# Self-attention scores of a query block: high and low keys in one TensorE product, with the low part added by ScalarE and VectorE

## The chip, the cores and the metric

The kernel runs on one core of a Trainium2 chip. The time is that of one execution on the device in microseconds (us), and the number compared is the median of several runs. The profile is of one more execution of the same program.

## The reference

One pre-norm decoder layer on x of 16 sequences of 256 tokens with 512 features: self-attention, cross-attention to a context, and a mixture of eight experts, each added to its input. The change lies in the self-attention:

```
x  = x + attn(layernorm(x), w_q, w_kv, w_dense)
q  = (x @ w_q)  as 4 groups x 4 heads x 128;   k, v = split(x @ w_kv) as 4 groups x 128
scores = q . k * 128**-0.5, causal;   probs = softmax(scores)
out = (probs @ v) @ w_dense
```

All of it is float32.

## The kernel before

`attention_phase` does the self-attention. To keep float32 accuracy with TensorE's float32r products, each operand is held as a high part (the value rounded to float32r by a ScalarE copy) and a low part (value minus high part, by VectorE), and each product is three: high·high, high·low, low·high (`product3`). The names end in `_h` and `_l`: `kT_h`, `qT_l` and so on.

The tokens go in blocks of 512, that is two sequences, and the heads in two halves. So there are 16 iterations `t`: 8 blocks with the first eight heads, then the same 8 blocks with the other eight. The first eight iterations also load the next block (`x_in`), normalise it and transpose it (`row_stats`, `mean_and_variance`, `apply_norm`, `xT_fill`). Iterations 7 ("turn") and 8 ("fresh") also load and split the second half's weights. Each iteration has 16 units `u`, a unit being one head of one sequence: 256 units in all.

A unit has 256 queries as two blocks of 128, in one PSUM bank `ps_s[u % 2]` of 512 columns. Columns 0 to 127 are the scores of the first 128 queries against the first 128 keys (the rest is masked by causality anyway), columns 128 to 383 those of the second 128 queries against all 256 keys; the last 128 columns are unused. `scores` makes six products, three of 128 columns and three of 256, and a bf16 product with an identity (line 603) that adds the causal mask to both diagonal blocks and raises `s_filled`.

Then, for unit u, on the other engines:

- VectorE, `maxima`: waits for `s_filled`; the negated row maximum of the first block (line 427) and of the second (line 428); raises `max_done`.
- ScalarE, `exponentials`: the exponentials of the first block (line 312) and of the second (line 314) from PSUM into `probs`, with their row sums.
- VectorE, `normaliser`: reciprocal of the sums (line 435), and the scaling of the first block of `probs` (line 437). GpSimd scales the second block (line 278).
- TensorE, `transposes`: `probs` is transposed into `ps_pT` (line 619) once both are scaled.
- ScalarE copies the high part `pT_h` (line 307), VectorE makes `pT_l` (line 384, of which there are several users).
- TensorE, `values_product`: for two units at a time, probabilities times values into `ps_c`; ScalarE copies `cT_h` (line 319) and VectorE makes `cT_l`.

Every engine works through its own list in the order in which the program has it. For ScalarE the body of unit u is: exponentials(u); for odd u up to 11 query ((u + 3) / 2), line 303, and for odd u from 3 context ((u − 3) / 2), line 319; then the copy `pT_h` of unit u − 1. For VectorE it is: maxima(u); in the first eight iterations a piece of the next block's layer norm (the statistics of `x_in`, line 389, in u = 3 to 6); normaliser(u); for the same odd u `qT_l` (line 420) and `cT_l`; then `pT_l` of unit u − 1; for u from 12 an add of the dense product. For TensorE it is: scores(u); half of the query projection number u // 2 + 2 while that is below 8, so for u up to 11; for odd u from 3 values_product; transposes(u − 1); for u from 12 a quarter of the dense product. After unit 15 come the keys, the values and the first two queries of the next block between the rest of the dense product, and the scores of unit 0.

So in unit u the exponentials of u are followed on ScalarE by `pT_h` of u − 1, VectorE's `pT_l` of u − 1 stands ahead of the maxima of u + 1, and these release the exponentials of u + 1.

Of the kernel before, what the change touches and what calls it, by code (L numbers as in the profile page):

```python
# [13 lines left out]
F32R = mybir.dt.float32r  # L14
BF16 = mybir.dt.bfloat16
I32 = mybir.dt.int32
ACT = mybir.ActivationFunctionType
ALU = mybir.AluOpType
AX = mybir.AxisListType

P = 128
BANK = 512
LN_EPS = 1e-5
# [11 lines left out]
def attention_phase(nc, x_rows, w_q, w_kv, w_dense, xT_pairs, x1_rows, TOKENS, HIDDEN, SEQ, HEADS, GROUPS):  # L35
# [18 lines left out]
    with ExitStack() as ctx:  # L54
        def sb(name, shape, dt=F32):
            return ctx.enter_context(nc.sbuf_tensor(name, shape, dt))
# [4 lines left out]
        def sem(name):  # L61
            return ctx.enter_context(nc.semaphore("a_" + name))
# [12 lines left out]
        acc = sb("acc", [P, TB, HIDDEN])  # L75
        xn = sb("xn", [P, TB, HIDDEN])
        xT = [sb(f"xT_{s}", [P, KT, BANK], F32R) for s in "hl"]
        kT = [sb(f"kT_{s}", [P, G, BANK], F32R) for s in "hl"]
        v = [sb(f"v_{s}", [P, TB, G * D], F32R) for s in "hl"]
        qT = [sb(f"qT_{s}", [P, 4, BANK], F32R) for s in "hl"]  # L80
        probs = sb("probs", [P, 2, 3 * P])
# [6 lines left out]
        mv = sb("mv", [P, TB, 2])  # L88
        veps = sb("veps", [P, TB])
        minus_half = sb("minus_half", [P, TB])  # L90
        negmax = sb("negmax", [P, 2, 2])
        rowsum = sb("rowsum", [P, 2, 2])
        rinv = sb("rinv", [P, 2, 2])
# [13 lines left out]
        stored = sem("stored")  # L107
        stats_done = sem("stats_done")
        aggr_done = sem("aggr_done")
        veps_done = sem("veps_done")  # L110
        rstd_done = sem("rstd_done")
        xn_done = sem("xn_done")
        xT_stored = sem("xT_stored")
        xT_loaded = sem("xT_loaded")
# [1 line left out]
        proj_high = sem("proj_high")  # L116
        proj_low = sem("proj_low")
        s_filled = sem("s_filled")
        max_done = sem("max_done")
        exp_done = sem("exp_done")  # L120
        rinv_done = sem("rinv_done")
# [79 lines left out]
        with nc.Block() as block:  # L201
# [49 lines left out]
            @block.gpsimd  # L251
            def _(pool):
                nc.gpsimd.memset(ident[:], 0.0).then_inc(consts, 1)
                nc.gpsimd.memset(causal[:], 0.0).then_inc(consts, 1)
                nc.gpsimd.memset(minus_half[:], -0.5).then_inc(consts, 1)
                pool.wait_ge(consts, 3)
                nc.gpsimd.affine_select(out=ident[:], in_=ident[:], compare_op=ALU.not_equal, fill=1.0, base=0,
                                        pattern=[[-1, P]], channel_multiplier=1).then_inc(consts, 1)

                nc.gpsimd.affine_select(out=causal[:], in_=causal[:], compare_op=ALU.is_ge, fill=NEG, base=0,  # L260
                                        pattern=[[-1, P]], channel_multiplier=1).then_inc(consts, 1)
                pool.wait_ge(consts, 5)
                nc.gpsimd.tensor_copy(ident_b[:], ident[:]).then_inc(consts, 1)

                def norm_scale(t):

                    wait_alone(pool, aggr_done, TB * (t + 1), (consts, 6))
                    nc.gpsimd.tensor_scalar(veps[:], mv[:, :, 1], LN_EPS, None, ALU.add).then_inc(veps_done, 1)
                    pool.wait_ge(veps_done, t + 1)
                    nc.gpsimd.tensor_tensor(veps[:], veps[:], minus_half[:], ALU.pow).then_inc(rstd_done, 1)  # L270

                norm_scale(0)

                def body(t, kind, half):
                    for u in range(UNITS):
                        s = u % 2
                        wait_alone(pool, rinv_done, UNITS * t + u + 1, (consts, 6))
                        nc.gpsimd.tensor_scalar(probs[:, s, P:3 * P], probs[:, s, P:3 * P], rinv[:, s, 1:2], None,  # L278
                                                ALU.mult).then_inc(probs_done, 1)
                        if u == TB + 3 and made(kind, half):  # L280
                            norm_scale(t + 1)

                pairs(body)(pool)

            @block.scalar
            def _(act):
# [18 lines left out]
                def probs_transposed(t, u):  # L305
                    act.wait_ge(pT_filled, UNITS * t + u + 1)
                    nc.scalar.activation(pT[0][:, u % 4, :], ps_pT[u % 2][:, 0:3 * P], ACT.Copy).then_inc(pT_high, 1)  # L307

                def exponentials(t, u):
                    s = u % 2  # L310
                    act.wait_ge(max_done, UNITS * t + u + 1)
                    nc.scalar.activation(probs[:, s, 0:P], ps_s[s][:, 0:P], ACT.Exp, bias=negmax[:, s, 0:1],  # L312
                                         accum_out=rowsum[:, s, 0:1])
                    nc.scalar.activation(probs[:, s, P:3 * P], ps_s[s][:, P:3 * P], ACT.Exp,  # L314
                                         bias=negmax[:, s, 1:2], accum_out=rowsum[:, s, 1:2]).then_inc(exp_done, 1)
# [19 lines left out]
                    values(0, n)  # L335
                query(0, 0)
                query(0, 1)
                exponentials(0, 0)

                def body(t, kind, half):  # L340
                    last = kind == "last"
                    for u in range(UNITS):
                        if u:
                            exponentials(t, u)
                        if u % 2 and (u + 3) // 2 < NH:
                            query(t, (u + 3) // 2)
# [25 lines left out]
                    if not last:  # L372
                        for n in range(2):
                            values(t + 1, n)
                        query(t + 1, 0)
                        query(t + 1, 1)
                        exponentials(t + 1, 0)

                pairs(body)(act)
# [2 lines left out]
            def _(dve):  # L382
# [12 lines left out]

                def apply_norm(t, n):
                    if n == 0:
                        dve.wait_ge(rstd_done, t + 1)
                    nc.vector.tensor_scalar(xn[:, n, :], x_in[:, n, :], mv[:, n, 0:1], veps[:, n:n + 1],
                                            ALU.subtract, ALU.mult).then_inc(xn_done, 1)  # L400

# [21 lines left out]

                def maxima(t, u):
                    s = u % 2
                    dve.wait_ge(s_filled, UNITS * t + u + 1)
                    nc.vector.tensor_reduce(negmax[:, s, 0:1], ps_s[s][:, 0:P], AX.X, ALU.max, negate=True)
                    nc.vector.tensor_reduce(negmax[:, s, 1:2], ps_s[s][:, P:3 * P], AX.X, ALU.max,  # L428
                                            negate=True).then_inc(max_done, 1)

                def normaliser(t, u):
# [107 lines left out]
            def _(pe):  # L539
# [50 lines left out]
                def scores(t, u):  # L590

                    m, b = unit(u)
                    g, s = m // HPG, u % 2
                    if b == 0:
                        pe.wait_ge(proj_low, FILLS * t + 8 + m + 1)
                    for qb in range(2):
                        c0, n = qb * P, (qb + 1) * P
                        q0 = b * SEQ + qb * P
                        product3(ps_s[s][:, c0:c0 + n], qT, (slice(None), m % 4, slice(q0, q0 + P)),
                                 kT, (slice(None), g, slice(b * SEQ, b * SEQ + n)), qb == 0, False)  # L600

                    diagonal = ps_s[s][:].rearrange("p (c k) -> p c k", c=BANK // P)[:, 0:3:2, :]
                    nc.tensor.matmul(diagonal, ident_b[:], causal[:, None, :].to_broadcast([P, 2, P]),
                                     start=False, stop=True).then_inc(s_filled, 1)

# [2126 lines left out]
```

## Time and profile before

| | |
|---|---|
| median of 3 runs | 2808.98 us |
| lowest and highest | 2804.44 and 2813.34 us |
| the profiled execution, its own time | 2802.59 us |
| span of its profile | 2801.0 us |
| self-attention in it | 0 to 1374 us |
| TensorE busy | 2603.9 us, 93% of the span |
| VectorE busy | 1875.0 us, 67% |
| ScalarE busy | 1455.1 us, 52% |
| GpSimd busy | 995.5 us, 36% |
| mean granted TensorE clock | 0.97 |

The engines are named in the rows as PE (TensorE's products), PEld (its weight loads), DVE (VectorE), ACT (ScalarE), POOL (GpSimd) and SP (SyncE, which issues DMAs). L427 is line 427 of the kernel. A row of the timeline has the start in us from the start of the span, the duration, the engine, the line, the operation and the tiles as output<-input, and in brackets the idle time of the engine before it and what ended that. Matmuls are pipelined: the next one starts before the shown end of the one before.

### The profile page before, as it was taken

Reading aid. Unit: us, or ns where it says so; the run is one execution under the profiler, and the core shown is the slowest. Engines: PE = TensorE matmul, PEld = TensorE weight load, DVE = VectorE, ACT = ScalarE, POOL = GpSimd, SP = SyncE. Lnnn points to the kernel's source line nnn. Section 1 sums busy time; section 2 is a strip of 40 time slices with the busy share of each in tenths; the row PEclk is TensorE's granted clock in tenths of the full one; section 3 lists DMA queues with packets and bytes.
Section 4 is the critical chain, followed back from the end, with each engine's and each line's share of the span. In section 5 each row is a group of like instructions: output and inputs, shape, how many; then the busy total and the mean of one; then the engine's idle time right before and its main releaser. Section 6 shows DMA issues by size and latency. Waiting matters only on the chain. (4 is left out here: it accounts for less than half of the span.)

```text
span 2801.0 us, 51111 instructions
## 1 busy us (share of the span) xinstructions
PE 2603.9 (93%) x15536; PEld 1816.8 (65%) x15537; DVE 1875.0 (67%) x3845; ACT 1455.1 (52%) x2868; POOL 995.5 (36%) x1178
## 2 busy tenths in 40 slices
PE   7999999999999999999759999999999986399997
PEld 6888888888888888888524444444443423277775
DVE  6556655566544455554569898889888876576665
ACT  4334433345433344333337777777777765255554
POOL 1112211112111112211235665665665647433332
PEclk9999999999999999999879999999999988699999
DMA  4102222013201111111154555555655558655554
GB/s 150 69 7 75 75 75 75 26 49 136 91 31 61 45 45 60 60 47 43 53 123 118 133 136 136 139 131 136 139 135 130 133 147 287 230 101 106 111 106 83
DMA packets 140817, 282.49 MB, mean 101 GB/s; under 512 B 39344, under 2 KB 42288, under 8 KB 135616
## 3 DMA queue, kind: packets, MB, share of 16 engines
q1 hardware_dynamic: 112416, 214.99, 26.7%
q0 software_dynamic: 23664, 58.09, 10.0%
q10 hardware_dynamic: 4656, 8.40, 1.0%
q8 instruction: 43, 0.70, 0.1%
q14 instruction: 38, 0.31, 0.0%
HBM read 147.82 MB, written 81.68 MB: 82 GB/s over the span
## 5 line engine op out<-in xcount | busy, mean ns | idle before, releaser
L1566 DVE TENSOR_REDUCE b_negmax<-b_ps_s 128x2 f32<-128x1024 f32 x512 | 611.2, 1218 | 52.9 <-PE b_ps_s L1751 46.4
L278 POOL TENSOR_SCALAR probs<-probs,rinv 128x256 f32<-128x256 f32 x256 | 242.0, 945 | 1094.3 <-DVE rinv L435 1094.3
L1366 ACT ACTIVATE b_probs<-b_ps_s 128x1024 f32<-128x1024 f32 x512 | 520.0, 1020 | 198.9 <-PE b_ps_s L1762 197.6
L312 ACT ACTIVATE probs<-ps_s,negmax 128x128 f32<-128x128 f32 x256 | 94.1, 367 | 484.5 <-DVE negmax L428 484.5
L1775 PE MATMUL b_ps_o<-b_probs,b_v_stack 128*32 128x256 f32 (+1 forms) x2816 | 295.0, 491 | 0.9 <-ACT b_probs L1366 0.8
L1762 PEld LDWEIGHTS b_ps_s<-b_stack 56*128 56x128 f32 x1024 | 96.3, 184 | 272.4 <-issue 165.7
L1762 PE MATMUL b_ps_s<-b_stack 56*128 56x512 f32 x1024 | 257.6, 500 | 15.4 <-DVE b_negmax L1566 7.5
L1751 PE MATMUL b_ps_s<-b_stack 54*128 54x512 f32 x1024 | 228.7, 443 | 42.4 <-DMA b_stack<-b_split 24.0
L543 PE MATMUL ps_proj<-xT_h,wq_h 128*128 128x512 f32 x512 | 216.0, 422 | 0.0
L2461 POOL DMA_INDIRECT out<-e_y,e_place_int x71 | 118.1, 1664 | 253.4 <-DMA out<-e_y,e_place_int 218.4
L543 PE MATMUL ps_proj<-xT_h,wq_l 128*128 128x512 f32 x512 | 201.7, 394 | 0.0
L543 PE MATMUL ps_proj<-xT_l,wq_h 128*128 128x512 f32 x512 | 200.1, 391 | 0.0
L435 DVE RECIPROCAL rinv<-rowsum 128x2 f32<-128x2 f32 x256 | 42.3, 165 | 217.5 <-ACT probs L314 217.5
L543 PE MATMUL ps_d<-wd_h,cT_h 128*128 128x512 f32 x384 | 157.6, 410 | 1.4 <-DVE cT_l L384 1.4
L1751 PEld LDWEIGHTS b_ps_s<-b_stack 54*128 54x128 f32 x1024 | 99.5, 190 | 91.6 <-ACT b_probs L1366 46.1
L543 PE MATMUL ps_s<-kT_h,qT_h 128*128 128x128 f32 (+1 forms) x512 | 156.8, 306 | 0.0
L543 PE MATMUL ps_d<-wd_h,cT_l 128*128 128x512 f32 x384 | 150.7, 392 | 0.0
L543 PE MATMUL ps_d<-wd_l,cT_h 128*128 128x512 f32 x384 | 150.0, 391 | 0.0
L543 PE MATMUL ps_s<-kT_l,qT_h 128*128 128x128 f32 (+1 forms) x512 | 142.8, 279 | 0.0
L307 ACT ACTIVATE pT_h<-ps_pT 128x384 fp32r<-128x384 f32 x256 | 127.1, 496 | 29.9 <-PE ps_pT L619 29.9
L384 DVE TENSOR_TENSOR pT_l<-ps_pT,pT_h 128x384 fp32r<-128x384 f32 x256 | 140.6, 549 | 2.5 <-ACT pT_h L307 2.5
L543 PE MATMUL ps_s<-kT_h,qT_l 128*128 128x128 f32 (+1 forms) x512 | 142.2, 278 | 0.0
(334 smaller groups left out, 6641.1 us busy)
## 6 DMA issues: line engine op xcount, KB each, us to landing
b_stack<-b_split SPq DMA_DIRECT2D x336, 128.0 KB
e_row<-rows_by_expert SPq DMA_DIRECT2D x71, 258.0 KB, 2.9
b_out_tiles<-row_sum_inverses SPq DMA_DIRECT2D x64, 256.0 KB
x<-acc SPq DMA_DIRECT2D x15, 1024.0 KB, 4.8
x_in<-in_x SPq DMA_DIRECT2D x8, 1024.0 KB, 8.1
normalised_x_split<-xT_h SPq DMA_DIRECT2D x8, 1024.0 KB, 9.8
normalised_x_split<-xT_l SPq DMA_DIRECT2D x8, 1024.0 KB, 11.0
acc<-in_x SPq DMA_DIRECT2D x8, 1024.0 KB, 11.3
```

What stands on the lines that cost most here:

```text
L278: nc.gpsimd.tensor_scalar(probs[:, s, P:3 * P], probs[:, s, P:3 * P], rinv[:, s, 1:2], None, ALU.mult).then_inc(probs_done, 1)
L307: nc.scalar.activation(pT[0][:, u % 4, :], ps_pT[u % 2][:, 0:3 * P], ACT.Copy).then_inc(pT_high, 1)
L312: nc.scalar.activation(probs[:, s, 0:P], ps_s[s][:, 0:P], ACT.Exp, bias=negmax[:, s, 0:1], accum_out=rowsum[:, s, 0:1])
L384: return nc.vector.tensor_tensor(dst, ps, h.bitcast(F32), ALU.subtract)
L435: nc.vector.reciprocal(rinv[:, s, :], rowsum[:, s, :]).then_inc(rinv_done, 1)
L543: ins = nc.tensor.matmul(out, w[a][w_at], m[b][m_at], start=st, stop=en)
L1366: nc.scalar.activation(probs[:, k % 2, p, :, :], ps[:], ACT.Exp, scale=0.25).then_inc(e_done, 1)
L1566: nc.vector.tensor_reduce(negmax[:, k, p, :], ps[:], AX.X, ALU.max, negate=True).then_inc(m_reduced, 1)
L1751: ins = nc.tensor.matmul(ps[:, i, :], stack[rows, quad, 0, p, k * P:(k + 1) * P], stack[rows, quad, 1, p, :], start=True, stop=True)
L1762: ins = nc.tensor.matmul(ps[:, i, :], stack[rows, q, 1, p, k * P:(k + 1) * P], stack[rows, q, 0, p, :], start=True, stop=True)
L1775: ins = nc.tensor.matmul(ps_o[32 * h:32 * h + 32, cols], v_stack[:, k, HQ * q + h, :], probs[:, k % 2, h // 2, h % 2, cols], start=(k == 0 ...
L2461: nc.gpsimd.indirect_dma_start(out, bass.IndirectOffsetOnAxis(place_int[i][:], 0), y[i][:], None, compute_op=ALU.add).then_inc(y_out[i], 16)
```

## The change

The high and the low keys become the two halves of one tensor, `kT_both`. For the first 128 queries the products high queries · high keys and high queries · low keys are one product of 256 columns, whose output goes to block 0 and to the unused block 3 of the bank (`blocks[:, 0:4:3, :]`). Low queries · high keys is added to block 0 as before. A score group so has five products and the mask where it had six and the mask.

The two blocks are added outside TensorE. ScalarE copies block 3 to SBUF (`by_low`) as soon as the group is done; VectorE adds it to block 0 into `first_scores_sum` in SBUF, then takes the maximum of the second block, then that of the sum; the first exponential reads the sum from SBUF and no longer PSUM. A semaphore `first_block` counts the copy and the add. VectorE waits for ScalarE's copy where it waited for TensorE. To make room for that semaphore `veps_done` and `rstd_done`, of the layer norm, become one, `rstd_step`.

```
-        kT = [sb(f"kT_{s}", [P, G, BANK], F32R) for s in "hl"]
+        kT_both = sb("kT", [P, 2, G, BANK], F32R)
+        kT = [kT_both[:, i] for i in range(2)]
...
+        by_low = sb("by_low", [P, 2, P])
+        first_scores_sum = sb("first_scores_sum", [P, 2, P])
...
+                def products_by_low(t, u):
+                    s = u % 2
+                    act.wait_ge(s_filled, UNITS * t + u + 1)
+                    nc.scalar.activation(by_low[:, s, :], ps_s[s][:, 3 * P:], ACT.Copy).then_inc(first_block, 1)
+
                 def exponentials(t, u):
                     s = u % 2
                     act.wait_ge(max_done, UNITS * t + u + 1)
-                    nc.scalar.activation(probs[:, s, 0:P], ps_s[s][:, 0:P], ACT.Exp, bias=negmax[:, s, 0:1],
+                    nc.scalar.activation(probs[:, s, 0:P], first_scores_sum[:, s, :], ACT.Exp, bias=negmax[:, s, 0:1],
                                          accum_out=rowsum[:, s, 0:1])
...
                         if u:
+                            products_by_low(t, u)
                             exponentials(t, u)
...
                 def maxima(t, u):
                     s = u % 2
-                    dve.wait_ge(s_filled, UNITS * t + u + 1)
-                    nc.vector.tensor_reduce(negmax[:, s, 0:1], ps_s[s][:, 0:P], AX.X, ALU.max, negate=True)
-                    nc.vector.tensor_reduce(negmax[:, s, 1:2], ps_s[s][:, P:3 * P], AX.X, ALU.max,
+                    dve.wait_ge(first_block, 2 * (UNITS * t + u) + 1)
+                    nc.vector.tensor_tensor(first_scores_sum[:, s, :], ps_s[s][:, 0:P], by_low[:, s, :], ALU.add).then_inc(first_block, 1)
+                    nc.vector.tensor_reduce(negmax[:, s, 1:2], ps_s[s][:, P:3 * P], AX.X, ALU.max, negate=True)
+                    dve.wait_ge(first_block, 2 * (UNITS * t + u) + 2)
+                    nc.vector.tensor_reduce(negmax[:, s, 0:1], first_scores_sum[:, s, :], AX.X, ALU.max,
                                             negate=True).then_inc(max_done, 1)
...
-                    for qb in range(2):
-                        c0, n = qb * P, (qb + 1) * P
-                        q0 = b * SEQ + qb * P
-                        product3(ps_s[s][:, c0:c0 + n], qT, (slice(None), m % 4, slice(q0, q0 + P)),
-                                 kT, (slice(None), g, slice(b * SEQ, b * SEQ + n)), qb == 0, False)
-
-                    diagonal = ps_s[s][:].rearrange("p (c k) -> p c k", c=BANK // P)[:, 0:3:2, :]
+                    blocks = ps_s[s][:].rearrange("p (c k) -> p c k", c=BANK // P)
+                    q0 = b * SEQ
+                    nc.tensor.matmul(blocks[:, 0:4:3, :], qT[0][:, m % 4, q0:q0 + P], kT_both[:, :, g, q0:q0 + P], start=True, stop=False)
+                    nc.tensor.matmul(blocks[:, 0, :], qT[1][:, m % 4, q0:q0 + P], kT[0][:, g, q0:q0 + P], start=False, stop=False)
+                    product3(ps_s[s][:, P:3 * P], qT, (slice(None), m % 4, slice(q0 + P, q0 + 2 * P)),
+                             kT, (slice(None), g, slice(q0, q0 + 2 * P)), False, False)
+
+                    diagonal = blocks[:, 0:3:2, :]
```

## Rows read from the trace of the kernel before

**Rows 1.** The page of the profiled execution, its head and its part 1.
```profile
span 2801.0 us, 51111 instructions
...
PE 2603.9 (93%) x15536; PEld 1816.8 (65%) x15537; DVE 1875.0 (67%) x3845; ACT 1455.1 (52%) x2868; POOL 995.5 (36%) x1178
...
```

**Rows 2.** Timeline, ScalarE, iteration 11: start us, us, engine, line, operation, tiles.
```profile
...
993.36 0.37 ACT L312 ACTIVATE probs<-ps_s,negmax 128x128 f32<-128x128 f32 x1 [1.48 <-DVE negmax L428]
...
994.16 0.49 ACT L307 ACTIVATE pT_h<-ps_pT 128x384 fp32r<-128x384 f32 x1
995.82 0.37 ACT L312 ACTIVATE probs<-ps_s,negmax 128x128 f32<-128x128 f32 x1 [1.17 <-DVE negmax L428]
...
996.62 0.59 ACT L303 ACTIVATE qT_h<-ps_proj 128x512 fp32r<-128x512 f32 x1
...
999.57 0.37 ACT L312 ACTIVATE probs<-ps_s,negmax 128x128 f32<-128x128 f32 x1 [1.48 <-DVE negmax L428]
...
```

**Rows 3.** Timeline, VectorE, the same stretch.
```profile
...
994.71 0.55 DVE L384 TENSOR_TENSOR pT_l<-ps_pT,pT_h 128x384 fp32r<-128x384 f32 x1
995.17 0.28 DVE L427 TENSOR_REDUCE negmax<-ps_s 128x1 f32<-128x128 f32 x1
995.37 0.41 DVE L428 TENSOR_REDUCE negmax<-ps_s 128x1 f32<-128x256 f32 x1
...
997.25 0.69 DVE L420 SCALAR_TENSOR_TENSOR qT_l<-ps_proj,qT_h 128x512 fp32r<-128x512 f32 x1
997.86 0.68 DVE L384 TENSOR_TENSOR cT_l<-ps_c,cT_h 128x512 fp32r<-128x512 f32 x1
998.46 0.55 DVE L384 TENSOR_TENSOR pT_l<-ps_pT,pT_h 128x384 fp32r<-128x384 f32 x1
998.92 0.28 DVE L427 TENSOR_REDUCE negmax<-ps_s 128x1 f32<-128x128 f32 x1
...
```

**Rows 4.** Timeline, TensorE, the products of u = 12 and the next transposes.
```profile
...
1009.20 0.31 PE L543 MATMUL ps_s<-kT_h,qT_h 128*128 128x128 f32 x1
1009.35 0.27 PE L543 MATMUL ps_s<-kT_l,qT_h 128*128 128x128 f32 x1
...
1009.57 0.34 PE L543 MATMUL ps_s<-kT_h,qT_h 128*128 128x256 f32 x1
1009.74 0.28 PE L543 MATMUL ps_s<-kT_l,qT_h 128*128 128x256 f32 x1
...
1009.98 0.28 PE L603 MATMUL ps_s<-causal,ident_b 128*128 128x256 bf16 x1
1010.61 0.52 PE L619 MATMUL ps_pT<-ident,probs 128*128 128x128 f32 x3 [0.35 <-POOL probs L278]
...
```

**Rows 5.** Timeline, TensorE, the mask product of u = 1.
```profile
...
976.81 0.28 PE L603 MATMUL ps_s<-causal,ident_b 128*128 128x256 bf16 x1
...
```

**Rows 6.** Timeline, VectorE, the first maximum of u = 1.
```profile
...
977.13 0.29 DVE L427 TENSOR_REDUCE negmax<-ps_s 128x1 f32<-128x128 f32 x1 [1.48 <-PE ps_s L603]
...
```

**Rows 7.** Timeline, ScalarE, exponentials of u = 1 and of u = 11.
```profile
...
977.79 0.37 ACT L312 ACTIVATE probs<-ps_s,negmax 128x128 f32<-128x128 f32 x1 [6.33 <-DVE negmax L428]
...
1008.24 0.37 ACT L312 ACTIVATE probs<-ps_s,negmax 128x128 f32<-128x128 f32 x1 [1.17 <-DVE negmax L428]
...
```

**Rows 8.** Timeline, GpSimd, the scaling of u = 11.
```profile
...
1009.52 0.94 POOL L278 TENSOR_SCALAR probs<-probs,rinv 128x256 f32<-128x256 f32 x1 [1.52 <-DVE rinv L435]
...
```

**Rows 9.** Waits of iterations 1 to 14: in total us, times, longest us.
```profile
...
DVE stats L389 <- DMA x_in<-in_x: 9.3, 6, 1.7
...
```

**Rows 10.** Timeline, ScalarE, iteration 4: exponentials of u 3 and 4.
```profile
...
389.52 0.37 ACT L312 ACTIVATE probs<-ps_s,negmax 128x128 f32<-128x128 f32 x1 [1.17 <-DVE negmax L428]
...
394.28 0.37 ACT L312 ACTIVATE probs<-ps_s,negmax 128x128 f32<-128x128 f32 x1 [2.50 <-DVE negmax L428]
...
```

**Rows 11.** Groups by shape, ScalarE: xcount, busy us, mean ns, idle before.
```profile
...
L1353 ACT ACTIVATE b_split<-b_raw_q 128x512 fp32r<-128x512 f32 x32 | 19.8, 618 | 0.7 <-DVE b_raw_q L1548 0.6
...
```

**Rows 12.** Groups by line and shape, VectorE, whole span.
```profile
...
L2198 DVE TENSOR_REDUCE r_rank<-c_above 128x32 f32<-128x256 f32 x8 | 3.4, 420 | 0.3
...
```

More of the change, by code:

```diff
@@ L109, in attention_phase @@
         aggr_done = sem("aggr_done")
-        veps_done = sem("veps_done")
-        rstd_done = sem("rstd_done")
+        rstd_step = sem("rstd_step")
         xn_done = sem("xn_done")
@@ L118, in attention_phase @@
         s_filled = sem("s_filled")
+        first_block = sem("first_block")
         max_done = sem("max_done")
@@ L267, in norm_scale @@
                     wait_alone(pool, aggr_done, TB * (t + 1), (consts, 6))
-                    nc.gpsimd.tensor_scalar(veps[:], mv[:, :, 1], LN_EPS, None, ALU.add).then_inc(veps_done, 1)
-                    pool.wait_ge(veps_done, t + 1)
-                    nc.gpsimd.tensor_tensor(veps[:], veps[:], minus_half[:], ALU.pow).then_inc(rstd_done, 1)
+                    nc.gpsimd.tensor_scalar(veps[:], mv[:, :, 1], LN_EPS, None, ALU.add).then_inc(rstd_step, 1)
+                    pool.wait_ge(rstd_step, 2 * t + 1)
+                    nc.gpsimd.tensor_tensor(veps[:], veps[:], minus_half[:], ALU.pow).then_inc(rstd_step, 1)
                 norm_scale(0)
@@ L337, in _ @@
                 query(0, 1)
+                products_by_low(0, 0)
                 exponentials(0, 0)
@@ L376, in body @@
                         query(t + 1, 1)
+                        products_by_low(t + 1, 0)
                         exponentials(t + 1, 0)
@@ L397, in apply_norm @@
                     if n == 0:
-                        dve.wait_ge(rstd_done, t + 1)
+                        dve.wait_ge(rstd_step, 2 * (t + 1))
                     nc.vector.tensor_scalar(xn[:, n, :], x_in[:, n, :], mv[:, n, 0:1], veps[:, n:n + 1],
```

## Prediction

> **What bounds the kernel now.** The page gives TensorE 93% of the span, and it is tempting to stop there [rows 1]. The change touches only self-attention (0 to 1374 us), 256 units in 16 iterations t of 16 units u, so I read the timeline of one iteration engine by engine and asked of each start what had just ended. A matmul of 512 columns is shown as 0.39 us long but the next one starts after 0.23, so a TensorE that waits 0.1 us still looks busy; its share proves nothing here.
>
> In the middle of an iteration, ScalarE and VectorE hand work to each other with no gap. From the exponential of u = 6 at 993.36, pT_h of u = 5 starts on ScalarE 0.80 later [rows 2]; VectorE's pT_l starts 0.55 after that, and the maxima of u = 7 follow 0.46 after it, with no idle time in their row, so the product had long been there [rows 3]; the exponential of u = 7 starts 0.65 after the first maximum [rows 2]. That is 2.46 us. The other half of the cycle is longer by the query and the context: exponential, 0.80 to qT_h, 0.63 to qT_l, 0.61 to cT_l, 0.60 to pT_l, 0.46 to the maxima, 0.65 to the exponential of u = 8, together 3.75 [rows 2, 3]. Every step is either the same engine's next instruction or starts about 0.05 us after the other engine's end. In iteration 11 the exponential of u = 1 starts at 977.79 and that of u = 11 at 1008.24 [rows 7], ten steps: 3.15 (u = 2), 2.46 five times, 3.75 four times, which is exactly these 30.45. The same steps stand in all 16 iterations, plus weight work in t = 7 and 8 and one stall named below.
>
> TensorE waits for this cycle: after the products of u = 12 it idles 0.35 us until GpSimd has scaled the probabilities of u = 11 [rows 4, 8]. From those transposes on (dense, projections, units 13 to 15, and units 0 and 1 of the next iteration) TensorE sets the pace: the maxima of u = 1 wait 1.48 us for its product and start 0.04 us after its end [rows 5, 6]. So an iteration is a TensorE stretch (from the transposes of u = 11 to the product of u = 1) and a ScalarE-VectorE stretch (from there to GpSimd's end for u = 11), one after the other.
>
> **The change part by part.** *TensorE.* One 128-column product of six goes, and the high one gets 256 columns. Products of 128 and of 256 columns follow each other at 0.11 to 0.17 us [rows 4]; the spacing is nearly that of the weight load, so the wider one costs what the narrow one did and a slot of 0.11 us goes. Bounds: 0 (if the two split blocks stream more slowly) to 0.15, the largest first spacing. I take 0.11, since the mask product with two split blocks is no slower than a plain one of 256 columns (0.28 us both) [rows 4]. It counts only where TensorE sets the pace: units 13, 14, 15, 0 and 1, so −0.55 us an iteration. In the other eleven it lengthens TensorE's own spare time.
>
> *VectorE.* Before: maximum of 128, of 256, then the exponential, 0.20 + 0.45 = 0.65 us. After: an add of 128, the maximum of 256, the maximum of 128 last. VectorE goes on to the next instruction 0.20 us after the start of one of 128 elements and 0.46 after pT_l's 384, that is 0.13 per 128 elements and 0.07 for each instruction, so 0.33 for 256. An add reads PSUM and SBUF as pT_l does, so it takes 0.20. Then 0.33, then 0.28 + 0.035 to ScalarE: 0.845, that is +0.20 us [rows 2, 3]. The wait for the add's own count is over when the 256 maximum has issued. Bounds of the add: 0.13, its elements alone, and 0.29, a whole duration as L427's and nothing overlapped. It sits in the cycle, since VectorE goes straight from pT_l into it.
>
> *The first exponential* now reads SBUF. Nothing in the trace is an exponential of 128 elements from SBUF. A copy of 512 from SBUF takes 0.62 us [rows 11], from PSUM 0.59 [rows 2]: +0.03. The upper bound is 0.12, a third of the 0.37 it takes now; below, 0. I take 0.04, and put it into the cycle, because the second exponential is queued behind.
>
> *ScalarE's copy* (by_low) of 128 elements: 512 take 0.59, 384 take 0.49, so 128 take 0.29 [rows 2]. It stands behind pT_h(u−2) and before the exponential of u, where ScalarE idles 1.17 or 1.48 us [rows 2]. It can start 0.4 us after pT_h and ends with its signal at 0.75; VectorE is then in pT_l until 0.55 + 0.46 = 1.01. Cover 0.25 us, so nothing, from u = 2 on. Behind it in ScalarE's queue stand only the exponentials, which need the add anyway. For u = 1 there is no cover: the product ends, then copy 0.29 and signal 0.05, then the add: +0.34 once an iteration.
>
> *Moved or renamed:* kT as one tensor, rstd_step for two counts. Same instructions, same queues, no DMA of SP or GpSimd changes: nothing. GpSimd's 0.94 us scaling runs beside other VectorE work today and does so still.
>
> *A cover that shrinks.* In t = 1 to 6 VectorE waits for x_in in u = 3, 9.3 us in 6 waits [rows 9]; it makes the step to u = 4 longer than 3.75: 4.76 in t = 4 [rows 10], 1.08 on average over the six. The load starts after the last dense add, so it keeps its distance from the product of u = 1, and is 0.11 later against it. An extra delay of up to 1.19 us before u = 4 therefore costs nothing there.
>
> *Sum.* With 0.24 us in the cycle per unit (0.20 + 0.04), the stretch from u = 1 to u = 11 has it 11 times: 2.64, + 0.34 at u = 1, − 0.55 on TensorE: +2.43 us for an iteration. Ten iterations (0, 7 to 15) pay it in full: 24.3; in the last only three score groups are saved ahead of the end, +0.2. In six, the delay by u = 3 is 0.34 + 3 × 0.24 = 1.06 and vanishes in the stall: +1.37 each, 8.2. Together +33 us. The profiled execution took 2802.6 us (span 2801.0), 0.2% under the median 2809.0 of the three; added to the median: **2842 us**.
>
> *A rule weighed.* The maximum of 256 elements takes 0.420 us from SBUF [rows 12] and 0.41 from PSUM [rows 3]: here the source makes no difference. The Trainium skill, "VectorE: DVE Perf Modes", section on SBUF-source operations, gives 58 cycles of fixed cost from SBUF and 120 from PSUM, so the last maximum would be 0.065 us cheaper, an estimate from that page; the sum would be 10 us less. By the rows it is not.
>
> **Rivals.** *TensorE is the bound after all* (the other side): its share of the span, and the lack of any listed wait at most units, speak for it; the gapless 2.46 and 3.75 against. Then 256 × 0.11 = 28 us go: 2781. It decides if the steps of the cycle are hidden slack, that is, if maxima could be delayed by 0.24 us without the next exponential moving. 7 in 100.
> *No net change:* VectorE's and ScalarE's additions are all but hidden (0.05 us or less in the cycle), so the slot won on TensorE pays for them: within 8 us of 2809. 6 in 100.
> *The last maximum is cheap, having SBUF as its source:* if it saves the 0.07 us that each instruction takes beyond its elements, ten iterations lose 11 × 0.07 = 0.77 of their loss and six (where three of the eleven lie before the stall) 0.56: 2831. The maximum of 256 from SBUF speaks against it [rows 12]. This is what the Trainium skill's page "VectorE: DVE Perf Modes" would have. 9 in 100.
> *No overlap around the add:* its full 0.29 and so 0.33 in the cycle: ten at 0.34 + 3.63 − 0.55 = 3.4 and six at 2.2: 2856. 12 in 100.
> *The copy is exposed:* if ScalarE's copy ends after pT_l on VectorE has, up to 0.34 us more enters each of 160 units: +54, 2896. It decides once the copy ends more than 0.25 us later than I reckon; a product that is late would do it. Against it: the maxima start without waiting for the product from u = 2 on. 8 in 100.
> *The forecast:* 58 in 100.
>
> **How the numbers follow.** The bounds of the cycle term are 0.13 (add 0.13, exponential 0) and 0.41 (0.29 and 0.12): +15 and +62 us by the same sum, 2824 and 2871. A saving of nothing on TensorE would add 9. The range 2822 to 2866 takes in the forecast with its likely errors, the cheap maximum and the missing overlap, and leaves out the exposed copy, the gain and most of no change. A change under 0.3% (8 us) can't be told from none. Faster 0.07, same 0.06, slower 0.87.
>
> **What would show each step.** Score groups on TensorE with five products and the mask, 0.11 us shorter. ScalarE's copy of 128 at 0.29 us right behind pT_h. On VectorE pT_l, add, maximum, maximum, exponential with 0.46, 0.20, 0.33, 0.32 between starts, and steps of about 2.70 and 3.99 us from exponential to exponential. TensorE's wait for GpSimd before the transposes of u = 11 grows, from 0.35 to over a microsecond, or moves to the waits for pT_l. VectorE's wait for x_in nearly goes. Outside self-attention nothing moves. The prediction is wrong if the steps stay 2.46 and 3.75, or if VectorE waits for the copy at most units.

## The result and the profile after

The changed kernel takes 2860.3 us (median of 4 runs, 2855.8 to 2864.3), the kernel before 2810.5 beside it: a ratio of 1.018, 95% interval 1.0155 to 1.0204, so 50 us slower. The forecast was 2842, range 2822 to 2866. The direction holds, and the mechanism as far as self-attention goes. The rise is 50 us where 33 were forecast, and what is missing lies where the forecast had nothing.

The page of the changed kernel, first lines and TensorE's instruction queue in part 3; below it the same queue of the kernel before:

```profile
span 2862.9 us, 51528 instructions
...
PE 2605.7 (91%) x15280; PEld 1788.9 (62%) x15281; DVE 1925.2 (67%) x4101; ACT 1517.7 (53%) x3124; POOL 997.3 (35%) x1178
...
q8 instruction: 87, 1.43, 0.2%
```

```profile
q8 instruction: 43, 0.70, 0.1%
```

The span is 61.9 us longer in this pair of profiles. TensorE has 256 products fewer and is busy 1.8 us more than before [rows 1], so nearly all of the added time is idle time of TensorE. The queue has twice the packets: TensorE fetched instructions that it did not fetch before.

Where the 61.9 us lie is read from the first instruction of each later phase. Timeline, GpSimd's first of cross-attention and TensorE's first of the experts, before and after:

```profile
1376.75 0.20 POOL L1167 MEMSET b_ident<- 128x128 f32 x1 [19.81 <-POOLq L201]
```

```profile
2424.55 1.11 PE L2603 MATMUL e_ps_x<-c_ident,e_row 128*128 128x128 f32 x4 [32.87 <-DMA e_row<-rows_by_expert]
```

```profile
1411.05 0.20 POOL L1181 MEMSET b_ident<- 128x128 f32 x1 [20.66 <-POOLq L204]
```

```profile
2486.75 1.12 PE L2617 MATMUL e_ps_x<-c_ident,e_row 128*128 128x128 f32 x4 [32.84 <-DMA e_row<-rows_by_expert]
```

Self-attention ends 34.3 us later (1411.05 − 1376.75), which is what was forecast (33). Cross-attention and the routing take 27.9 us more (1075.7 for 1047.8), in code that the change does not touch. The experts take as long as before.

**Self-attention.** Iteration 11 on ScalarE, from the copy of u = 1 to the exponential of u = 8 (answers to [rows 2, 7]):

```profile
998.59 0.28 ACT L315 ACTIVATE by_low<-ps_s 128x128 f32<-128x128 f32 x1 [5.22 <-PE ps_s L617]
999.75 0.40 ACT L320 ACTIVATE probs<-first_scores_sum,negmax 128x128 f32<-128x128 f32 x1 [0.88 <-DVE negmax L441]
...
1016.45 0.40 ACT L320 ACTIVATE probs<-first_scores_sum,negmax 128x128 f32<-128x128 f32 x1 [1.51 <-DVE negmax L441]
...
1017.30 0.48 ACT L310 ACTIVATE pT_h<-ps_pT 128x384 fp32r<-128x384 f32 x1
1017.67 0.27 ACT L315 ACTIVATE by_low<-ps_s 128x128 f32<-128x128 f32 x1
1019.14 0.40 ACT L320 ACTIVATE probs<-first_scores_sum,negmax 128x128 f32<-128x128 f32 x1 [1.19 <-DVE negmax L441]
...
1023.12 0.40 ACT L320 ACTIVATE probs<-first_scores_sum,negmax 128x128 f32<-128x128 f32 x1 [1.51 <-DVE negmax L441]
```

VectorE between the exponentials of u = 6 and u = 7 (answers to [rows 3]):

```profile
1017.84 0.55 DVE L395 TENSOR_TENSOR pT_l<-ps_pT,pT_h 128x384 fp32r<-128x384 f32 x1
1018.30 0.28 DVE L438 TENSOR_TENSOR first_scores_sum<-ps_s,by_low 128x128 f32<-128x128 f32 x1
1018.50 0.41 DVE L439 TENSOR_REDUCE negmax<-ps_s 128x1 f32<-128x256 f32 x1
1018.83 0.28 DVE L441 TENSOR_REDUCE negmax<-first_scores_sum 128x1 f32<-128x128 f32 x1
```

From exponential to exponential it is 2.69 and 3.98 us, where it was 2.46 and 3.75 [rows 2]. pT_l, add, maximum, maximum, exponential start 0.46, 0.20, 0.33 and 0.31 us apart. The first exponential takes 0.40 us and not 0.37, and what follows it on ScalarE starts 0.85 us after it and not 0.80. The copy (0.27 us) starts 0.37 after pT_h and is over 0.35 before the add: covered. At u = 1 it is not: it waits for TensorE and the exponential starts 1.16 us after the copy.

TensorE, the products of u = 10 and its waits (answers to [rows 4]):

```profile
1026.57 0.36 PE L611 MATMUL ps_s<-kT,qT_h 128*128 128x256 f32 x1
...
1027.25 0.28 PE L617 MATMUL ps_s<-causal,ident_b 128*128 128x256 bf16 x1
...
1034.88 0.52 PE L633 MATMUL ps_pT<-ident,probs 128*128 128x128 f32 x3 [0.68 <-POOL probs L281]
```

The table of waits, 100 to 1300 us, for TensorE, for x_in and, after, for the copy (answers to [rows 9]):

```profile
PE ps_c L543 <- DVE pT_l L384: 7.6, 10, 2.4
...
PE ps_pT L619 <- POOL probs L278: 5.2, 15, 0.4
```

```profile
PE ps_c L556 <- DVE pT_l L395: 40.4, 70, 3.1
...
DVE first_scores_sum L438 <- ACT by_low L315: 35.8, 51, 1.7
...
PE ps_pT L633 <- POOL probs L281: 12.9, 17, 1.6
...
DVE stats L400 <- DMA x_in<-in_x: 4.8, 6, 0.9
```

From the wide product to the mask it is 0.68 us, where six products took 0.78. TensorE gives this back in waiting: it waits for pT_l 70 times (10 before), and 0.68 us for GpSimd before the transposes of u = 11 (0.35 before). VectorE waits for ScalarE's copy 51 times in these 1200 us, which have some 220 units, so not at most units.

**Cross-attention.** TensorE around the jump back at the end of one pass of the loop, the changed kernel:

```profile
1639.78 0.40 PE L1693 MATMUL b_ps_p<-b_c_h,b_wk_l 128*128 128x512 f32 x1
1642.59 0.49 PE L1776 MATMUL b_ps_s<-b_stack 56*128 56x512 f32 x2 [2.41 <-issue]
```

The same kernel in windows of 10 us (busy time and instructions of each engine, then the granted clock, DMA share, GB/s):

```profile
1630.00:1640.00 10.00, 9.88 (x76) 4.18 (x74) 8.64 (x10) 8.80 (x11) 8.71 (x11) 1.00 0.64 153
1640.00:1650.00 10.00, 7.59 (x35) 2.59 (x36) 5.86 (x7) 4.26 (x5) 7.05 (x11) 0.70 0.28 73
```

"issue" means that nothing which the profile shows held it. This pause comes five times, 2.3 to 2.7 us each, every 110 to 113 us; two sequences are one pass. The loop has six passes and so five jumps back to its start, and in the trace each pause lies just behind one of these jumps. The granted clock is 0.70 in the 10 us from 1640, where it was 1.00 in the 10 us before. TensorE had been busy for 9.88 of those earlier 10 us, then stood still for 2.4 us and started again at 1642.59; from 1644.2 to 1651 us the granted clock is 0.51, so nearly all of that time is at its lower level, 1.2 GHz. The Trainium skill, page "Runtime: NRT & Kernel Launch", section "Instruction fetch mechanics", says that instructions are fetched ahead in blocks of 256 and that a taken branch to a block no longer held must wait for a fetch. The doubled packets and the pauses behind the jumps agree. The section also says that only two blocks are held at a time. The kernel before does not bear that out: one pass of this loop is 1627 instructions of TensorE in its trace, more than six such blocks, and it ran without these pauses and with 43 packets.

### The profile page after: what moved, and what is told of

Same layout as the page of the kernel before. It is cut to its first block and busy times, and to the rows that moved or that the text cites. A ratio compares the mean times of both kernels' runs of the same rounds, so it can differ in the third digit from the quotient of the medians.

```text
span 2862.9 us, 51528 instructions
## 1 busy us (share of the span) xinstructions
PE 2605.7 (91%) x15280; PEld 1788.9 (62%) x15281; DVE 1925.2 (67%) x4101; ACT 1517.7 (53%) x3124; POOL 997.3 (35%) x1178
## 5 line engine op out<-in xcount | busy, mean ns | idle before, releaser
L1776 PE MATMUL b_ps_s<-b_stack 56*128 56x512 f32 x1024 | 262.9, 509 | 26.4 <-issue 12.4
L320 ACT ACTIVATE probs<-first_scores_sum,negmax 128x128 f32<-128x128 f32 x256 | 103.1, 403 | 317.6 <-DVE negmax L441 317.6
L315 ACT ACTIVATE by_low<-ps_s 128x128 f32<-128x128 f32 x256 | 72.0, 281 | 148.6 <-PE ps_s L617 146.9
L633 PE MATMUL ps_pT<-ident,probs 128*128 128x128 f32 x768 | 126.0, 273 | 15.0 <-POOL probs L281 15.0
L556 PE MATMUL ps_c<-pT_h,v_h 128*128 128x512 f32 (+1 forms) x256 | 96.7, 378 | 46.1 <-DVE pT_l L395 46.1
L431 DVE SCALAR_TENSOR_TENSOR qT_l<-ps_proj,qT_h 128x512 fp32r<-128x512 f32 x128 | 88.4, 691 | 73.4 <-ACT qT_h L306 73.4
```

The costliest lines, as they stand in the source:

```text
L320: nc.scalar.activation(probs[:, s, 0:P], first_scores_sum[:, s, :], ACT.Exp, bias=negmax[:, s, 0:1], accum_out=rowsum[:, s, 0:1])
L556: ins = nc.tensor.matmul(out, w[a][w_at], m[b][m_at], start=st, stop=en)
L633: ins = nc.tensor.transpose(ps_pT[s][:, j * P:(j + 1) * P], probs[:, s, j * P:(j + 1) * P], ident[:])
L1776: ins = nc.tensor.matmul(ps[:, i, :], stack[rows, q, 1, p, k * P:(k + 1) * P], stack[rows, q, 0, p, :], start=True, stop=True)
```

## The experiments

Ratios are to the kernel before, run on the same chip beside each. It took 2812.0 us beside e1 to e4, 2819.0 beside e5 to e10 and 2818.8 beside e11 and e12. "Self-attention ends" is from here on the end of its last instruction: 1374.3 us in the kernel before, 1408.6 in the changed one.

### e1: the changed kernel, TensorE's instructions put back in place

```
                pe.wait_ge(consts, 6)
+                for _ in range(80):
+                    nc.tensor.matmul(ps_pT[0][:, 0:16], ident_b[:], ident_b[:, 0:16], start=True, stop=True)
```

> The changed kernel with 80 small products (16 columns, nobody reads them) on TensorE ahead of its first work, where it idles until 13.4 us. They bring TensorE's instructions in the cross-attention loop back to the places that they have in the kernel before; the data flow is that of the changed kernel. Theory: the profile of the changed kernel has 34 us more in self-attention and 28 us more in cross-attention, where nothing was changed but where TensorE fetches instructions anew in each pass of the loop and stands still for 2.4 us; with the places restored the fetches and the pauses go, cross-attention is back within 3 us of before, self-attention stays at 1408 to 1410 us, and the time is that of before plus 34: 2843 to 2846. Rival: cross-attention is slower for another reason (order of DMAs, placement in SBUF, semaphores), then nothing changes and it stays at about 2860.

Measured 2841.5 us, ratio 1.0112 (1.0092 to 1.0133): +31 us. TensorE's queue and the two phases:

```profile
q8 instruction: 43, 0.70, 0.1%
```

```profile
1410.83 0.20 POOL L1183 MEMSET b_ident<- 128x128 f32 x1 [20.79 <-POOLq L204]
```

```profile
2460.80 1.11 PE L2619 MATMUL e_ps_x<-c_ident,e_row 128*128 128x128 f32 x4 [33.78 <-DMA e_row<-rows_by_expert]
```

The packets are 43 again, no pause is left, and cross-attention and routing take 1050.0 us. Self-attention keeps its 34 us. The data flow is that of the changed kernel, so 19 of the 50 us (1.018 − 1.0112, of 2811; by the two intervals some 10 to 28) are the places of TensorE's instructions and not the scores. In the pair of profiles it is 25.7 us, and 24.6 of them lie between the first and the last jump of the loop: 560.3 us in the changed kernel, 535.7 in e1, 535.3 in the kernel before. What is left, +31 us, is near the 33 that the forecast gave to self-attention alone.

### e2: the kernel before, TensorE's instructions moved

The same products at the same place in the kernel before, 48 of them.

```
+                for _ in range(48):
```

> The kernel before with 48 such products ahead, which put TensorE's cross-attention loop at the same place within a block of 256 instructions as in the changed kernel. Theory of the instruction fetch: self-attention stays at 1374 us, cross-attention gets 12 to 28 us longer with pauses of TensorE of about 2.4 us once in a pass of the loop, 2822 to 2838. Rival: places of instructions do not matter, 2810 as before.

Measured 2824.7, ratio 1.0053 (1.0036 to 1.0070): +15 us. Queue, and the waits from 1594 us to 2206:

```profile
q8 instruction: 88, 1.44, 0.2%
```

```profile
PE b_ps_s L1764 <- issue: 9.6, 6, 2.3
```

From the first to the last jump of the loop it is 550.4 us, 15.1 more than in the kernel before. A loss of the same kind comes in a kernel without any part of the change.

### e3: ScalarE's and VectorE's part alone

```
-                    nc.tensor.matmul(blocks[:, 0:4:3, :], qT[0][:, m % 4, q0:q0 + P], kT_both[:, :, g, q0:q0 + P], start=True, stop=False)
+                    nc.tensor.matmul(blocks[:, 0, :], qT[0][:, m % 4, q0:q0 + P], kT[0][:, g, q0:q0 + P], start=True, stop=False)
+                    nc.tensor.matmul(blocks[:, 3, :], qT[0][:, m % 4, q0:q0 + P], kT[1][:, g, q0:q0 + P], start=False, stop=False)
```

> Only the ScalarE and VectorE part of the change: TensorE keeps six products, high by high to block 0 and high by low to block 3 each of 128 columns; copy, add and maxima as in the changed kernel. TensorE has as many instructions as before. Theory (the cycle of ScalarE and VectorE bounds units 2 to 12): steps of the exponentials of 2.69 and 3.98 us as in the changed kernel, self-attention 34 + 16 x 0.57 = 43 us longer than before, 1417; cross-attention as before; time 2853. Rival (TensorE is the bound and the wide product costs what it saves): self-attention at or below 1409.

Measured 2848.5, ratio 1.0134 (1.0115 to 1.0153): +38 us. Timeline, ScalarE, u = 6 to 8 of iteration 11:

```profile
1022.72 0.40 ACT L320 ACTIVATE probs<-first_scores_sum,negmax 128x128 f32<-128x128 f32 x1 [1.51 <-DVE negmax L441]
...
1025.41 0.40 ACT L320 ACTIVATE probs<-first_scores_sum,negmax 128x128 f32<-128x128 f32 x1 [1.20 <-DVE negmax L441]
...
1029.39 0.40 ACT L320 ACTIVATE probs<-first_scores_sum,negmax 128x128 f32<-128x128 f32 x1 [1.50 <-DVE negmax L441]
```

The steps are those of the changed kernel, 2.69 and 3.98, though TensorE has its six products: its work does not enter them. Self-attention ends at 1416.1 us, 7.5 later than in the changed kernel (1408.6); 9 was expected. The steadier measure is TensorE's stretch from the transposes of u = 11 to the mask product of the next u = 1: in iterations 8 to 14 it takes 49.1 us in the kernel before and in e3, and 48.5 in the changed kernel and in e4.

### e4: the wide product alone

```
-                    nc.scalar.activation(probs[:, s, 0:P], first_scores_sum[:, s, :], ACT.Exp, bias=negmax[:, s, 0:1],
+                    nc.scalar.activation(probs[:, s, 0:P], ps_s[s][:, 0:P], ACT.Exp, bias=negmax[:, s, 0:1],
...
```

products_by_low and the add are gone too, the maxima are those of the kernel before, and 80 small products stand ahead as in e1. The product of high queries and low keys of the first block is so left out of the scores.

> Only TensorE's part of the change: one product of 256 columns for the high queries with high and low keys, five products a group; ScalarE and VectorE as before, from block 0 alone. It leaves out high queries by low keys of the first 128 queries. 80 small products ahead keep the places of the instructions in cross-attention. Theory: steps of the exponentials stay 2.46 and 3.75; only the five score groups between the transposes of u = 11 and the product of u = 1 count, 0.57 us an iteration: self-attention 9 us shorter, 1365, time 2801. Rival (TensorE bounds all units): 256 x 0.11 = 28 us shorter, 2782.

Measured 2803.0, ratio 0.9977 (0.9965 to 0.9990): −6.5 us. Timeline, ScalarE, u = 1 and u = 11 of iteration 11:

```profile
972.35 0.37 ACT L320 ACTIVATE probs<-ps_s,negmax 128x128 f32<-128x128 f32 x1 [6.10 <-DVE negmax L436]
...
1002.85 0.37 ACT L320 ACTIVATE probs<-ps_s,negmax 128x128 f32<-128x128 f32 x1 [1.17 <-DVE negmax L436]
```

Ten steps take 30.50 us, with 30.45 before [rows 7]. So 256 slots of 0.11 us taken from TensorE are worth 6.5 us (1 to 10 by the interval), and not 28: "TensorE is the bound" falls. Self-attention ends at 1369.3 us, 5.0 earlier where 9 was expected. The last exponential starts 7.8 us earlier, but from there to the end of self-attention the granted clock is 0.85 on average in this profile and 1.00 in that of the kernel before.

### e5: the sum kept in PSUM

The add writes block 0 back, and the last maximum and the first exponential read it there; 80 products ahead as in e1.

```
-                    nc.vector.tensor_tensor(first_scores_sum[:, s, :], ps_s[s][:, 0:P], by_low[:, s, :], ALU.add).then_inc(first_block, 1)
+                    nc.vector.tensor_tensor(ps_s[s][:, 0:P], ps_s[s][:, 0:P], by_low[:, s, :], ALU.add).then_inc(first_block, 1)
```

> The changed kernel (places of the instructions restored as in the first of these runs, which took 2841.5) with the sum written back into block 0 in PSUM, so that the last maximum and the first exponential read PSUM. Theory: a first exponential from SBUF costs 0.04 to 0.05 us of the cycle per unit (0.84 to 0.85 us from exponential to the next copy, where before had 0.80); from PSUM the steps are 2.65 and 3.93 and the time falls by 11 x 16 x 0.04 = 7 us to 2834. The Trainium skill's page VectorE: DVE Perf Modes gives a fixed cost 62 cycles smaller for VectorE from SBUF: by it the last maximum would get 0.065 us dearer in PSUM and the time would rise by 4 us. Rival: the source of the exponential makes no difference, 2841.

Measured 2845.1 us beside a kernel before at 2819.0, ratio 1.0085 (1.0057 to 1.0113); e1 had 1.0112. About 7 us less was expected; the intervals overlap, so the traces have to say it:

```profile
1003.77 0.37 ACT L320 ACTIVATE probs<-ps_s,negmax 128x128 f32<-128x128 f32 x1 [1.20 <-DVE negmax L441]
...
1004.58 0.60 ACT L306 ACTIVATE qT_h<-ps_proj 128x512 fp32r<-128x512 f32 x1
...
1007.72 0.37 ACT L320 ACTIVATE probs<-ps_s,negmax 128x128 f32<-128x128 f32 x1 [1.51 <-DVE negmax L441]
...
1010.38 0.37 ACT L320 ACTIVATE probs<-ps_s,negmax 128x128 f32<-128x128 f32 x1 [1.20 <-DVE negmax L441]
```

Steps of 3.95 and 2.66, 0.03 less than in the changed kernel; the exponential takes 0.37 us again and 0.81 pass to the next copy. VectorE's 0.84 from add to exponential stays. Self-attention ends at 1403.4 us, 5 earlier. SBUF as the source costs ScalarE 0.03 to 0.04 us here; VectorE's maximum of 128 takes 0.28 from either, so the 62 cycles of difference that the Trainium skill gives ("VectorE: DVE Perf Modes", section on SBUF-source operations) do not show.

### e7: the kernel before, maxima first for even u

```
+                EARLY = range(2, 13, 2)
...
-                        if u:
+                        if u and u not in EARLY:
                             maxima(t, u)
...
+                        if u + 1 in EARLY:
+                            maxima(t, u + 1)
                         if u >= 1:
                             pT_low_part(t, u - 1)
```

> The kernel before, with one change of order on VectorE: for even u from 2 to 12 the maxima of u stand ahead of the low part of the transposed probabilities of u - 2 and not behind it. No work is added or removed. Theory: the cycle of ScalarE and VectorE is 2.46 + 3.75 - 0.46 = 5.75 us for two units, less than TensorE's 6.10; TensorE becomes the bound, the steps become 2.5 and 3.6, the wait of TensorE of 0.35 us for GpSimd before the transposes of u = 11 goes, and an iteration gets 0.5 us shorter (1.0 where x_in is late): 8 to 14 us less, 2798 to 2804. Rival (TensorE bounds the kernel anyway): no difference, 2811.

Measured 2804.7 beside 2819.0, ratio 0.9946 (0.9925 to 0.9967): −15 us. ScalarE's exponentials of u = 6 to 8 in iteration 11, and TensorE's waits:

```profile
977.97 0.37 ACT L312 ACTIVATE probs<-ps_s,negmax 128x128 f32<-128x128 f32 x1 [0.91 <-DVE negmax L428]
...
980.59 0.37 ACT L312 ACTIVATE probs<-ps_s,negmax 128x128 f32<-128x128 f32 x1 [1.15 <-DVE negmax L428]
...
984.07 0.37 ACT L312 ACTIVATE probs<-ps_s,negmax 128x128 f32<-128x128 f32 x1 [0.91 <-DVE negmax L428]
```

```profile
PE ps_pT L623 <- POOL probs L278: 2.1, 3, 1.2
...
PE ps_c L547 <- DVE pT_l L384: 0.7, 1, 0.7
```

No work was added or removed; pT_l no longer stands between the query's and context's low parts and the maxima of even units. Two units take 6.10 us where they took 6.21, and TensorE's waits for pT_l and for GpSimd fall from 12.8 us to 2.8. Self-attention ends at 1358.1 us, 16.2 earlier. (Cross-attention and routing take 1074.2 us in this one profile, 26 more than in that of the kernel before, with 43 packets and no pause in the loop. This phase differs that much between profiles without any fetched loop, so a single pair of profiles does not settle a difference in it.)

### e8: the changed kernel, maxima first for even u

The same edit, in e1's kernel.

```
-                        if u:
+                        if u and u not in EARLY:
                             maxima(t, u)
```

> The changed kernel, places restored, with the same change of order. Theory: the cycle falls from 2.69 + 3.98 = 6.67 to 6.20 us for two units, still above TensorE's 5.88; five such pairs an iteration, 2.3 us, less some of the x_in stall that comes back in six iterations: 33 us less than 2841, that is 2808, about the kernel before. Rival (the loss is work on ScalarE, not the cycle): 2841 stays.

Measured 2817.3 beside 2819.0, ratio 0.9995 (0.9980 to 1.0009): no difference to the kernel before, and 33 us less than e1 by the ratios, as expected. ScalarE, u = 6 to 8 of iteration 11:

```profile
994.22 0.40 ACT L320 ACTIVATE probs<-first_scores_sum,negmax 128x128 f32<-128x128 f32 x1 [1.04 <-DVE negmax L441]
...
996.90 0.40 ACT L320 ACTIVATE probs<-first_scores_sum,negmax 128x128 f32<-128x128 f32 x1 [1.19 <-DVE negmax L441]
...
1000.42 0.40 ACT L320 ACTIVATE probs<-first_scores_sum,negmax 128x128 f32<-128x128 f32 x1 [1.04 <-DVE negmax L441]
```

Two units take 6.20 us where the changed kernel has 6.67. Self-attention ends at 1376.1 us, 32 earlier than with the old order. The work that the change adds is all still there, so its mere amount is not what cost 31 us in e1. But it is not free with the new order either: against e7, which has that order without the change, e8 is 14 us slower by the ratios, and its self-attention ends 18 us later. The add and the dearer exponential still stand in the cycle; what left it is pT_l, once in two units.

### e10: order, and the wide product only where TensorE sets the pace

As e7, with wide product, copy and add in units 0, 13, 14 and 15 alone, and 20 small products ahead.

```
+    WIDE = (0, 13, 14, 15)
...
+                    if u in WIDE:
+                        act.wait_ge(s_filled, UNITS * t + u + 1)
+                        nc.scalar.activation(by_low[:, s, :], ps_s[s][:, 3 * P:], ACT.Copy).then_inc(first_block, 1)
...
+                    if u in WIDE:
+                        nc.tensor.matmul(blocks[:, 0:4:3, :], qT[0][:, m % 4, q0:q0 + P], kT_both[:, :, g, q0:q0 + P], start=True, stop=False)
+                        nc.tensor.matmul(blocks[:, 0, :], qT[1][:, m % 4, q0:q0 + P], kT[0][:, g, q0:q0 + P], start=False, stop=False)
```

> The kernel before with the maxima of even u first, and with the wide product, ScalarE's copy and the add only in units 0, 13, 14 and 15, where TensorE sets the pace and the longer way to the exponentials is covered; places of the instructions kept. Theory: what the change of order gives (8 to 14 us) and 4 x 0.11 x 16 = 7 us besides: 2790 to 2796. Rival: the longer way is not covered in units 13 to 15 (TensorE waits for GpSimd's probabilities there), then no better than the order alone.

Measured 2793.3 beside 2819.0, ratio 0.9911 (0.9890 to 0.9933): −25 us, the best kernel of this study. Self-attention ends at 1350.7 us (before 1374.3, e7 1358.1). The intervals of e7 and e10 just touch. In the profiles self-attention is 7.4 us shorter than in e7, which is 64 slots of 0.115 us: in these four units TensorE sets the pace, and the longer way to the exponentials is covered.

### e11 and e12: where the instruction fetch turns

The products of e1 again, 20 ahead of the changed kernel (e11) and 24 ahead of the kernel before (e12).

```
-                for _ in range(80):
+                for _ in range(20):
```

> The changed kernel with 20 small products ahead in place of 80. Counting a product as two instructions (weight load and product) and 256 to a block, TensorE's cross-attention loop then runs from block 22.07 to 27.05; in the kernel before it is 22.54 to 27.52 and in the changed kernel 21.92 to 26.90. Theory: the loop is kept when its end lies early or midway in a block and fetched anew in each pass when it lies near the block's end, where the fetch ahead has already taken one block more. Then no new fetches: 43 packets on TensorE's instruction queue and not 87, about 2842. Rival: what matters is another distance from the places before, or the exact places; then 87 packets and about 2860.

> The kernel before with 24 small products ahead: the loop of cross-attention runs from block 22.73 to 27.71. With the kernel before (end at 0.52 of a block, kept) and the shifted one (0.89, fetched anew) it narrows the edge down: kept means 43 packets and 2811, fetched anew 87 or 88 packets and about 2825. I lean to kept; nothing that the runs show so far decides it.

e11 (two runs): 2881.3 us, ratio 1.0216 (1.0171 to 1.0261), and 87 packets: the expectation was wrong. Two pauses a pass now, ten in 1594 to 2206 us:

```profile
PE b_ps_o L1791 <- issue: 13.0, 5, 3.1
PE b_ps_s L1778 <- issue: 11.8, 5, 2.9
```

e12: 2814.9, ratio 0.9987 (0.9969 to 1.0006), 43 packets: kept. The positions in the two expectations hold as differences only: they rest on a count of 1275 instructions in the loop, while the trace has 1627 in a pass, since each probabilities-times-values product of the program is two there. Told as the number of instructions ahead of the loop, against the kernel before: 0 and 48 more, and it is kept; 96 more (e2), 120 fewer (e11) and 160 fewer (the changed kernel), and it is fetched anew. In the blocks of 256 of the page named above, 160 fewer is the same place as 96 more. Where between 48 and 96 the edge lies, and why, stays open.

## Why the prediction was right, and where it fell short

**The bound** was right. e4 takes 0.11 us from every unit on TensorE and leaves the ten steps as they were (30.50 us for 30.45); e3 gives TensorE its old work and has the new steps; e7 shortens the cycle without removing any work and gains.

**VectorE's term** (+0.20 us per unit, 0.845 from add to exponential): measured 0.84. **The exponential from SBUF** (+0.04): 0.05 in what follows it in the changed kernel, 0.03 in the step by e5. Together 0.24 was put into the cycle, and the steps grew by 0.23.

**ScalarE's copy** (covered from u = 2, +0.34 at u = 1) was right. From the product's end the exponential of u = 1 starts 1.20 us later and not 0.69, that is +0.51 for the 0.54 forecast. One exception was missed. In iterations 7 and 8 ScalarE splits weights behind pT_h of u = 5, and the copy of u = 7 stands behind that. Timeline, ScalarE, iteration 7:

```profile
668.14 0.40 ACT L320 ACTIVATE probs<-first_scores_sum,negmax 128x128 f32<-128x128 f32 x1 [1.50 <-DVE negmax L441]
...
669.37 1.05 ACT L333 ACTIVATE wkv_h<-wkv_raw 128x1024 fp32r<-128x1024 f32 x1
670.31 0.28 ACT L315 ACTIVATE by_low<-ps_s 128x128 f32<-128x128 f32 x1
671.47 0.40 ACT L320 ACTIVATE probs<-first_scores_sum,negmax 128x128 f32<-128x128 f32 x1 [0.88 <-DVE negmax L441]
```

VectorE waits for the copy there (0.54 us), and the step to u = 7 is 3.33 us, 0.64 over the usual 2.69; in iteration 8 it is 4.18 where it was 2.98. Together 1.6 us.

**TensorE's term** (−0.55 an iteration in five score groups): the TensorE stretch is 0.57 us shorter; e4's 6.5 us and e3's difference of 7.5 to the changed kernel are near its 9 us over 16 iterations. That makes 0.11 us a slot; the rows of u = 10 show 0.10.

**The x_in stall** was forecast to nearly vanish; it halved. VectorE's wait is 4.8 us after 9.3 [rows 9], and an iteration of the first half grew by 1.56 us on average and not 1.37; one of the second half by 2.25 and not 2.43. The errors of the terms cancel: that it is 34 us for 33 is in part luck.

**The step that failed** is "Outside self-attention nothing moves". The change makes TensorE's code 160 instructions shorter ahead of the cross-attention loop, and at its new place the loop is fetched anew in each pass (87 packets for 43): 19 us of the 50, by e1. The step "same instructions, same queues: nothing" looked at DMA queues that move data, and no term was there for the one that moves code. The range held the result only because it was made wide for other errors, which is luck.

## What to carry to other kernels

Before an operation is moved from a busy engine to idle ones, follow one unit of the steady state from engine to engine by start times. Where each start is the end of the one before, that cycle is the likely bound, whatever the busy shares say, and the idle engine's new operation counts in full if it stands in it: VectorE's add did, ScalarE's copy beside it did not. Then the first thing to try is the order: an operation whose input has long been ready should not stand behind one that closes the cycle. And any edit that changes the number of instructions ahead of a large loop can move the loop: compare the packets of the instruction queues of both profiles before a difference is explained by the edit.

## What the runs showed of the hardware

The same program of TensorE, with a loop of 1627 instructions a pass, costs 43 packets on TensorE's instruction queue or 87 to 88, depending on how many instructions stand ahead of the loop. By the ratios that is 15 us (e2), 19 (the changed kernel) or 29 (e11 against e1) of some 2811. From the first to the last jump of the loop, five passes, the profiles have 535 to 543 us in all nine kernels with 43 packets, and 550.4 (e2), 560.3 (the changed kernel) and 579.3 (e11) in those with 87 or 88. The pauses themselves are 9.6, 12.4 and 24.8 us; the lower granted clock after a pause is where a part of the rest may lie, which was not measured by itself. Every kernel with 43 packets was free of these pauses in the loop, every one with 87 or 88 had them. Behind the loop, in the routing, single pauses of the same name come in five kernels with 43 packets too (one of about 3.1 us in each of e5, e7, e8, e10 and e12, and one of 13.4 us in e10); what sets those off was not looked for.
